# Two context attentions: a pair's second turns of probabilities, and its logits, moved behind the next pair's first scores

## What is computed

```
def xattn(x, ctx):                      # 16 heads of 16
    q = heads(layernorm(x) @ Wq + bq);  k = heads(ctx @ Wk + bk);  v = heads(ctx @ Wv + bv)
    s = q k^T / 4;  s = where(mask, s, low)
    return (softmax(s) v) @ Wo + bo
x = x + xattn(x, ctx)                   # then layernorm(x) @ router weights: the logits
```

## Time and profile before

| | |
|---|---|
| median of 3 runs | 1797.31 us (1793.06 to 1801.25) |
| profiled execution: its own time, its span | 1797.2 us, 1795.4 us |
| busy in the span: PE, DVE, ACT, POOL | 88%, 57%, 34%, 23% |
| context attention of layer 0, first product to last logits | 504 to 659 us |
| context attention of layer 1, first scores to last logits | 1329 to 1463 us |

### The profile page before, as it was taken

One profiled execution on the slowest core, in us unless ns is written; L12 is line 12 of the kernel. 1 busy time (PEld: TensorE's weight loads), 2 busy tenths in 40 slices (PEclk: granted clock), 3 DMA queues, 4 the chain that ended last, 5 costly groups with the idle time before them and its releaser, 6 DMA issues. The chain is left out here.

```text
span 1795.4 us, 29275 instructions
## 1 busy us (share of the span) xinstructions
PE 1580.8 (88%) x9415; PEld 1055.8 (59%) x9416; DVE 1021.3 (57%) x2024; ACT 601.7 (34%) x1167; POOL 409.8 (23%) x839
## 2 busy tenths in 40 slices
PE   6899999999969941899999999789988837999996
PEld 5433333333347731577777777646656627999996
DVE  6678888888549967311112211378878854444443
ACT  3367777777735520111111111034445510000000
POOL 1000000000014410342222211156642212333332
PEclk9799999999989975899999999989999968999998
DMA  2112221111310120133223331200024115666664
GB/s 72 40 38 65 52 55 39 44 38 45 137 47 25 36 66 1 44 100 91 58 60 93 96 85 15 60 3 1 2 81 132 37 60 168 176 179 180 189 179 118
DMA packets 89222, 134.90 MB, mean 75 GB/s; under 512 B 17712, under 2 KB 66224, under 8 KB 88976
## 3 DMA queue, kind: packets, MB, share of 16 engines
q1 hardware_dynamic: 73968, 113.08, 20.0%
q0 software_dynamic: 15168, 20.72, 7.3%
HBM read 98.04 MB, written 20.84 MB: 66 GB/s over the span
## 5 line engine op out<-in xcount | busy, mean ns | idle before, releaser
L2101 DVE TENSOR_REDUCE mx<-ps 128x1 f32<-128x1024 f32 x256 | 306.2, 1217 | 58.1 <-PE ps L2210 58.1
L2000 ACT ACTIVATE turns_of_use<-ps 128x512 f32<-128x512 f32 x512 | 281.5, 596 | 130.9 <-PE ps L2217 128.8
L1285 PE MATMUL ps<-xTe,wide 128*128 128x320 f32 x1024 | 279.4, 435 | 1.0 <-issue 1.0
L1285 PEld LDWEIGHTS ps<-xTe,wide 128*128 128x128 f32 x1024 | 195.5, 191 | 82.1 <-issue 2.6
L1352 DVE TENSOR_TENSOR hTe<-prT,ps 128x320 f32<-128x320 f32 x128 | 62.5, 488 | 214.3 <-ACT prT L1324 205.7
L2217 PE MATMUL ps<-QS,KS 99*128 99x512 bf16 x512 | 163.2, 387 | 6.7 <-ACT turns_of_use L2000 4.7
L507 POOL TENSOR_TENSOR nv<-nv 128x2 f32<-128x2 f32 (+2 forms) x84 | 18.2, 216 | 641.7 <-DVE nv L692 637.3
L2210 PE MATMUL ps<-KS,QS 96*128 96x512 bf16 x512 | 144.4, 395 | 9.8 <-DVE mx L2101 6.9
L1442 PEld LDWEIGHTS ps<-xw_all,w1t 128*128 128x128 f32 x1248 | 145.9, 192 | 3.7 <-issue 0.9
L1442 PE MATMUL ps<-xw_all,w1t 128*128 128x128 f32 x1248 | 146.4, 276 | 1.2 <-ACT xw_all L1474 1.2
L1324 ACT ACTIVATE prT<-ps 128x320 f32<-128x320 f32 x128 | 56.0, 437 | 264.4 <-PE ps L1285 255.8
(11 more groups left out here) (313 smaller groups left out, 2152.8 us busy)
## 6 DMA issues: line engine op xcount, KB each, us to landing
w1t<-in_L_ffn_w SPq DMA_DIRECT2D x39, 1024.0 KB
wide<-in_L_ffn_gate_weight SPq DMA_DIRECT2D x8, 1024.0 KB
wide<-_L_ffn_ff_pre_act_weight SPq DMA_DIRECT2D x8, 1024.0 KB
wide<-L_ffn_ff_post_act_weight SPq DMA_DIRECT2D x8, 1024.0 KB
wide<-in_L_ffn_w SPq DMA_DIRECT2D x1, 8192.0 KB, 27.1
QS<-wide SPq DMA_DIRECT2D x192, 32.0 KB, 2.0
KS<-wide SPq DMA_DIRECT2D x192, 32.0 KB, 2.0
VS<-V_all SPq DMA_DIRECT2D x32, 128.0 KB, 2.1
```

The lines of the kernel that those rows point to most:

```text
L1285: ins = pe.matmul(ps[:, 3 + 2 * (q % 2) + n, 0:HC], wt[:, k, f * P:f * P + P], xTe[:, k, hf * HC:hf * HC + HC], start=(k == 0), stop=(k == ...
L2000: act.activation(PT[:, q % 8, :], ps[:, 4 + q % 2, :], ACT.Exp).then_inc(h_e.sem, 1)
L2101: v.tensor_reduce(mx[:, s, t:t + 1], ps[:, 2 * (t % 2):2 * (t % 2) + 2, :], AX.XY, ALU.max).then_inc(h_rm.sem, 1)
```

## The change

In both layers, on PE `turn_probs(U, 1)` and `logits` leave the end of their round and stand in the next round behind `scores(i, U, 0)`, ahead of `weigh`; the loop has one round more. `scores(i, U, 1)` goes ahead of `project_prev` in layer 0, and in layer 1 `pe_turn_in` goes ahead of it and `queries` ahead of `turn_probs(U, 0)`. On DVE `keep_logits` goes behind the softmax of half 0. On ACT the orders differ by layer from here on. `pe_bias` moves behind the turn out of the last pair. No instruction is added or taken away.

```diff
--- before.py
+++ after.py
@@ -632,18 +632,24 @@
                     prev_rows_turned(i + 2)
                 if i == -1 and layer == 0:
                     act.wait_ge(x_cr.sem, x_cr.upto(layer))
+                if layer == 0 and here(i):
+                    probs(of(layer, i), 0)
                 if here(i + 1) and (layer, i) != (1, -1):
                     act_rows_in(act, i + 1, of(layer, i + 1))
-                if here(i):
-                    probs(of(layer, i), 0)
                 if here(i + 1):
                     turned_in(of(layer, i + 1))
+                if layer == 1 and here(i):
+                    probs(of(layer, i), 0)
+                if layer == 1 and here(i - 2):
+                    rows_out(i - 2, of(layer, i - 2))
+                if layer == 1 and here(i + 1):
+                    queries(of(layer, i + 1))
                 if here(i):
                     probs_turned(of(layer, i), 0)
-                if here(i - 2):
+                if layer == 0 and here(i + 1):
+                    queries(of(layer, i + 1))
+                if layer == 0 and here(i - 2):
                     rows_out(i - 2, of(layer, i - 2))
-                if here(i + 1):
-                    queries(of(layer, i + 1))
                 if here(i):
                     probs(of(layer, i), 1)
                 if here(i - 2):
@@ -740,12 +746,12 @@
 
             for i in range(-2, NP + 3):
                 U = of(layer, i)
-                if here(i - 3):
-                    keep_logits(i - 3, U - 3)
                 if layer == 1 and i == 0:
                     scale_last()
                 if here(i):
                     softmax(i, U, 0)
+                if here(i - 3):
+                    keep_logits(i - 3, U - 3)
                 if layer == 1 and i == 0:
                     add_last()
                 if here(i - 1):
@@ -913,39 +919,43 @@
                                         prT[:, blk, :], start=True, stop=True)
                 ins.then_inc(x_av.sem, 1)
 
-            for i in range(-2, NP + 2):
+            for i in range(-2, NP + 3):
                 U = of(layer, i)
-                if layer == 0 and i == NP + 1:
-                    pe_bias(pe)
                 if i == -layer:
                     pe.wait_ge(x_cr.sem, x_cr.upto(layer))
                 if here(i):
                     scores(i, U, 0)
                 if here(i - 1):
+                    turn_probs(U - 1, 1)
+                if here(i - 3):
+                    logits(U - 3)
+                if here(i - 1):
                     weigh(i - 1, U - 1)
-                if layer == 0 and here(i + 2):
-                    if i + 2 > 0:
-                        turn_prev(i + 2)
-                    project_prev(i + 2)
+                if layer == 0 and 0 < i + 2 < NP:
+                    turn_prev(i + 2)
                 if left and i == 0:
                     left()
+                if layer == 1 and 0 < i + 1 < NP:
+                    pe_turn_in(pe, layer, i + 1)
                 if here(i):
                     scores(i, U, 1)
-                if here(i + 1) and (layer, i) != (1, -1):
+                if layer == 0 and here(i + 2):
+                    project_prev(i + 2)
+                if layer == 0 and here(i + 1):
                     pe_turn_in(pe, layer, i + 1)
+                if layer == 1 and here(i + 1):
+                    queries(U + 1)
                 if here(i):
                     turn_probs(U, 0)
-                if here(i + 1):
+                if layer == 0 and here(i + 1):
                     queries(U + 1)
                 if here(i - 1):
                     pe.wait_ge(x_no.sem, x_no.upto(U - 1))
                     out_rows(oT, xw["o"], OUT, x_wo)
                 if here(i - 2):
                     turn_out(i - 2, U - 2)
-                if here(i):
-                    turn_probs(U, 1)
-                if here(i - 2):
-                    logits(U - 2)
+                if layer == 0 and i == NP + 1:
+                    pe_bias(pe)
 
         def half_of(u):
 
```

## The result

The changed kernel takes 1784.68 us (median of 6 runs, 1781.47 to 1785.55) against 1797.57 us, a ratio of 0.9929 with a 95% interval of 0.9913 to 0.9945. Run again beside other runs of the kernel before it came to 1784.82 against 1794.84, 0.9946 (0.9926 to 0.9965). So the gain is 10 to 13 us, and the forecast was 10.2 (1787.0 us). Each ratio is made from all runs of a set, so it is not quite the quotient of the two medians.

The account below looks back on a forecast made before the run. PE and DVE were taken to wait for each other in a ring in layer 1, with DVE full in layer 0. 5.5 + 6.0 - 0.1 - 1.2 = 10.2 us off 1797.2 gives 1787.0 us, range 1781 to 1795.

Parts of the forecast that it names:

- Layer 1, pairs 3 to 6: Layer 1's steady pairs take 12.45 us instead of 13.82, 1.37 saved in each, 5.5 us for four.
- the chain: Layer 1, PE from the wait on `keep_logits` to the projection's end: DVE's addition starts at 10.15 instead of 9.7.
- the floor of 12.0: Shortest possible pair in layer 1: 13.82 us less DVE's three waits and the overlap at them.
- Layer 1, pairs 0 to 2: Layer 1's first pairs, with no wait on `keep_logits` yet, gain 6.0 us (bounds 4 and 7.3).
- The walk: Layer 1's first pairs traced in the new order: 3.3, 1.1 and 2.9 us saved, 7.3 at the full clock.
- a dip: PE at the low clock, 1.6 us in all; about one expected on the path in layer 1's first pairs.
- Layer 1, the end: Layer 1's pair 7 and end keep their order; `keep_logits` ahead of the normalisation costs 0.1 us.
- Layer 0: Whole of layer 0: start -0.2, pairs 3 to 5 -1.0, pair 6 +1.0, end -1.0, in sum -1.2 us.
- Pair 6: Layer 0's pair without `turn_prev`: 13.4 us on the new path instead of 14.88; +1.0 us taken.
- The bias: End of layer 0: `pe_bias` between the last turn and last logits takes 1.80 us at the low clock, -1.0 us.
- The rule on turns: Turns don't count as clock activity as products do; by it the low clock comes in each pair, 1806 us.
- The second rival, slower: Both layers: the clock falls in every pair, 1.6 us each on the path, 1806 us; chance 0.07.

Follow-up runs that it names:

- own bank: The changed kernel with layer 1's logits in a free bank of `ps` and no wait for their reading there: 1782.60 us, 0.9918 (0.9899 to 0.9937).
- early projection: The changed kernel with layer 1's `out_rows` ahead of `turn_probs(U, 0)`, the wait for the logits' reading kept: 1781.29 us against 1794.84, 0.9921.
- filled kernel before: The kernel before with four unread products between weighting and second scores in layer 1: 1794.60 us against 1797.99, 0.9985 (0.9969 to 1.0000).

## Why the prediction was right or wrong

- **Layer 1, pairs 3 to 6: 5.5 us, measured 5.3.** 12.45 was forecast, 12.51 came; the wait for the projection 0.45 and 0.47, the idle time ahead of the turn in 1.3 and 1.05. The own bank and the early projection confirm the chain, and the floor of 12.0 that was forecast came as 11.94.
- **Layer 1, pairs 0 to 2: 6.0 us, measured 8.8.** The mechanism was right: the idle time ahead of pair 1 fell from 5.07 us to 1.32 (2 was forecast). The term was too small, in two ways. The walk implied pairs of 11.5, 12.8 and 12.0 us, and 10.79, 12.20 and 11.86 came, 1.5 us less. And 1.3 us were taken off for a dip that neither profile of the changed kernel has. The caution had a ground, though: four other profiles of the new order have a dip in pair 0, with queries of 3.05 to 3.64 us instead of 1.99. Pair 0 stays at 10.8 us even so, since behind fast queries PE only waits 1.80 us for DVE, but pair 1 grows from 12.20 to between 12.75 and 12.96. Of the 8.8 us some 2.9 are the old order's own dips, as the filled kernel before shows in pairs 1 and 2 and the pair 0 of 13.9 in two profiles.
- **Layer 1, the end: -0.1, measured +2.7 and +0.4 in two profiles.** The clock of the single execution decides that. With the idle times filled the end takes 29.0 us in the old order and 29.1 and 29.9 in the new, so the order by itself gains nothing there.
- **Layer 0: -1.2.** The first pairs were forecast at -0.2 and came at -0.1, by the mechanism named (PE idles 3.40 us and then does the projection in 3.68). Pairs 3 to 5 cost 1.2 (forecast 1.0, and 14.74 for 14.7). Pair 6 gave 1.6, where 1.0 was taken and the walk had 13.4; it took 13.29, with PE waiting 0.84 us for ACT's rows. The bias was mis-sized: 0.7 us in four profiles and 0.2 in one instead of 1.0, because the logits behind it take 1.72 or 1.24 us instead of 1.88. That sums to -0.4 in most profiles. The rest of the 4.0 us that layer 0 lost in the first profile (1.9 in the second, by the sums of the table) is the slower start, 1.6, and in the first profile an end with PE at the low clock from its turns on. Over profiles the end is 34.3 us in the new order (six) and 32.6 in the old (four); the bias is part of that, and whether the new order invites the rest, the runs do not settle.
- **The rule on turns** gave no dip where it put one: with turns and logits together in each round and an idle time behind them (1.05 us in the changed kernel), PE's products in pairs 1 to 6 of layer 1 ran at the full clock in all nine profiles of the new order. The dips in pair 0 came behind an idle time of 2.18 us, ahead of any logits. The second rival, slower, is out.
- **The sum** of 10.2 lies between the two measurements, 12.9 and 10.0, and its closeness is partly luck. Its terms for the pairs add up to 11.3, and 14.4 came; those for the ends to -1.1, and 0.0 and -0.3 came; and the start, for which no term stood, lost 1.6 between the profiles, which is the clock's doing and not the change's.

## What to carry to other kernels

Walk one steady round of both engines from the starts in the trace, and put in every wait that moves with a moved instruction: that gave four periods to about 0.1 us (12.45 for 12.51, 14.7 for 14.74, 13.4 for 13.29, 12.0 for 11.94). It was worse at the first pairs, where nothing is steady: 0.7 and 0.6 us too long. Where two engines alternate, see whether the freed engine now waits for something that was moved behind the other's long operation, and give it its own buffer. Before crediting a gain to an order, look whether it lies in stretches at another clock, and take a second profile.

## What the runs showed of the hardware that I had not expected

Useless products paid. With TensorE's idle times behind the last pair filled, the kernel before fell from 1794.84 to 1789.86 us (0.9979, 0.9962 to 0.9995). The changed one with its own bank fell from 1782.60 to 1777.69, but in two sets of runs whose intervals overlap; there the rows carry the claim, with ends of 31.3 for 33.4 and 29.9 for 34.6 us. What shrank is PE's work at the lower clock (a projection of 3.78 us against 1.99) behind idle times of 2.3 to 2.5 us.

Such an idle time alone does not decide it. Idle times of 2.08 us in the middle of layer 1 were followed by full clock in pairs 3 to 6 and by dips in pairs 1 and 2, in three profiles alike, and those of 2.31 and 2.49 us at the end by full clock in one execution of the changed kernel and by the low clock in another. The Trainium skill, "TensorE: Matmul & The Clock Gate", section "HAM oscillation — how this bites in real kernels", describes falls behind idle times too, in a kernel whose waits for DMA of 3 to 5 us are longer than any of these. Its section "What's actually happening" says that the transition point varies from run to run. It says so of the rise at a kernel's start; the ends of 30.4 and 32.7 us from one kernel show that the fall varies too.
